# Ranking three quarters of the tokens early: seventeen expert tiles of layer 1 ahead of the last block's routing

## What is computed

```python
# attention half of layer 1: two-layer MLP behind the attention
h = relu(out @ W1 + b1); x = x + tanh(g_xattn[1]) * (h @ W2 + b2)
# expert half of layer 1, on xn = layernorm(x)
logits = xn @ Wg + bg
topk_vals, topk_idx = top_k(logits, 2)
topk_w = softmax(topk_vals)
h  = relu(xn @ W1[e] + b1[e])          # W1[e]: 256 x 512
eo = h @ W2[e] + b2[e]                 # W2[e]: 512 x 256
mixed = sum over the token's two experts of topk_w * eo
y = mixed + xn
x = x + tanh(g_ffn[1]) * (gamma * layernorm(y) + beta)
```

## Time and profile before

| | us |
|---|---|
| median of 3 runs | 1427.07 (1425.08 to 1428.34) |
| the profiled execution | 1421.31 |
| its span, first to last instruction | 1419.5 |
| TensorE busy | 1346.5 (95%) |
| ScalarE busy | 975.0 (69%) |
| VectorE busy | 597.7 (42%) |
| GpSimd busy | 175.8 (12%) |
| mean granted clock of TensorE | 0.986 |

### The profile page before, as it was taken

How to read it: one execution, slowest core, us unless ns; L and a number is a source line. 1 busy time by engine, 2 the same in 40 slices (tenths; PEclk the granted TensorE clock), 3 DMA queues, 4 the chain that set the end, 5 groups by cost and what they waited for, 6 DMA issues and landing times. The chain is left out here.

```text
span 1419.5 us, 33642 instructions
## 1 busy us (share of the span) xinstructions
PE 1346.5 (95%) x14020; PEld 741.4 (52%) x14020; DVE 597.7 (42%) x1257; ACT 975.0 (69%) x1190; POOL 175.8 (12%) x194
## 2 busy tenths in 40 slices
PE   7899999999999998999988999999999998899994
PEld 4433333333333555999953333334334338799973
DVE  7412143152333344334271222662662676544435
ACT  4699999999998233223268996996996980255532
POOL 2000000000000331233300000000000000276530
PEclk9999999999999999999999999999999999899997
DMA  7771010010100913311259110110111215022224
GB/s 212 176 124 29 21 28 21 25 25 17 32 24 21 312 66 96 123 49 50 74 123 197 39 28 17 35 29 17 35 29 50 68 35 175 27 72 72 72 69 162
DMA packets 66533, 101.96 MB, mean 72 GB/s; under 512 B 10476, under 2 KB 48626, under 8 KB 65484
## 3 DMA queue, kind: packets, MB, share of 16 engines
q1 hardware_dynamic: 60428, 83.53, 21.6%
q0 software_dynamic: 5952, 16.26, 3.6%
HBM read 69.04 MB, written 26.22 MB: 67 GB/s over the span
## 5 line engine op out<-in xcount | busy, mean ns | idle before, releaser
L1410 ACT ACTIVATE arena<-ps 128x1024 f32<-128x1024 f32 x536 | 535.3, 1195 | 37.1 <-PE ps L1123 36.5
L1123 PE MATMUL ps<-arena 99*32 99x512 bf16 x6528 | 450.0, 382 | 13.2 <-issue 6.4
L1123 PEld LDWEIGHTS ps<-arena 99*32 99x32 bf16 x6528 | 158.4, 95 | 384.6 <-issue 159.8
L1143 PE MATMUL ps<-arena 128*32 128x512 f32 x2240 | 355.8, 593 | 0.7 <-ACT xn L1403 0.4
L1410 ACT ACTIVATE wqkv<-ps 128x1024 f32<-128x1024 f32 x264 | 279.3, 1192 | 16.5 <-PE ps L1123 16.3
L1143 PE MATMUL ps<-wqkv,arena 128*32 128x512 f32 x1088 | 206.4, 593 | 0.1
L1508 DVE SCALAR_TENSOR_TENSOR work<-xn,last_v,ps 128x512 f32<-128x512 f32 x30 | 22.4, 748 | 307.3 <-PE ps L1143 307.2
L2005 PE MATMUL ps<-work,arena 128*128 128x128 f32 x1184 | 145.4, 279 | 3.0 <-DVE work L2097 1.6
L2005 PEld LDWEIGHTS ps<-work,arena 128*128 128x128 f32 x1184 | 144.3, 195 | 7.0 <-DVE work L2097 4.0
L1039 POOL DMA_INDIRECT work<-xn_img,fetch x62 | 60.4, 974 | 558.5 <-DVEq L1095 514.1
L2019 PE MATMUL ps<-arena,work 128*128 x496 | 117.2, 380 | 0.0
(11 more groups left out here) (228 smaller groups left out, 1289.3 us busy)
## 6 DMA issues: line engine op xcount, KB each, us to landing
arena<-in_ew SPq DMA_DIRECT2D x16, 512.0 KB, 5.8
arena<-q_img SPq DMA_DIRECT2D x32, 192.0 KB
arena<-y_tok SPq DMA_DIRECT2D x12, 512.0 KB, 6.5
arena<-k_img SPq DMA_DIRECT2D x8, 624.0 KB, 12.1
q_img<-work SPq DMA_DIRECT2D x18, 256.0 KB, 2.6
k_img<-work SPq DMA_DIRECT2D x21, 208.0 KB, 2.4
arena<-q_img SPq DMA_DIRECT2D x32, 128.0 KB
arena<-in_rg SPq DMA_DIRECT2D x8, 512.0 KB, 7.3
```

The lines of the kernel that those rows point to most:

```text
L1123: last = nc.tensor.matmul(ps[i * VW:(i + 1) * VW, buf + j, :], keys, q2[0:ROWS + SHIFT, h, :], start=True, stop=True, skip_group_check=True)
L1143: last = nc.tensor.matmul(ps[j * VW:(j + 1) * VW, 6 + g % 2, :], v_aug[:, c, HG * g + j, :], exps, start=(c == 0), stop=(c == NC - 1), ski ...
L1410: nc.scalar.activation(probs[n % RING], ps[:, buf:buf + 2, :], ACT.Exp, scale=SCALE).then_inc(s_exp, 1)
```

## The change

Layer 1 ranks the tokens of blocks 0 to 2 (24 of the 32 one-hot columns) by themselves. Of these 3072 pairs at least 24 - 7 = 17 tiles are full whatever the draw, and the first 17 full ones become tiles 0 to 16 of the loop. What is left over is ranked again, together with block 3, into 22 further tiles. The count of tiles stays 39.

- VectorE: in block 3 all eight experts' router products and `route` come before the third group; after it comes `rank_first`. `places` for the first lists follows the last group. `rank_rest` and its `places` follow the one-hots of block 3. Then the loop for tiles 17 to 38.
- TensorE: the first counts stand behind step 44 of block 3, the first lists behind attention, then 12 keep-warm products instead of 26, and after the projection the loop begins, in the same block. The last transpose, the last router product, the second counts and the second lists are put between tiles (after `down(0)`, `down(1)`, `down(3)` and `down(11)`). The other keep-warm products of layer 1 go.
- ScalarE: in tiles 0 to 16 it copies the rows, does bias and ReLU in four instructions per tile, and copies the result out (`first_scalar`), since VectorE is ranking. From tile 17 the loop is as before, but two diagonals follow each ReLU.
- GpSimd: in tiles 0 to 16 it adds the second bias. It fetches their rows from a second copy of the normalised rows, `xn_early`, of blocks 0 to 2.
- SP: writes that copy (three transfers of 512 KB), and loads `eb1` during the last block. The down weights are loaded where they were.

```diff
-FETCHED = [4, 1]
+FETCHED = [4, 0]
+COUNTS_AT = 44
...
+        self.early = self.top * (NB - 1) * TB if self.mlp else 0
+        self.first = self.early - E + 1 if self.mlp else 0
+        self.rest = self.tiles - self.first
...
-                    out=rows_in[i % ROWBUFS], out_offset=None, in_=xn_img[l],
+                    out=rows_in[i % ROWBUFS], out_offset=None, in_=xn_early if i < L.first else xn_img[l],
...
+            def first_scalar(act, between):
+                act.wait_ge(s_pl, 1)
+                act.wait_ge(s_eg, 16 * (E + 1))
+                copy_gate(act, 0)
+                copy_gate(act, 1)
...
+                def hidden(i):
+                    e = act.value_load(tile_e[0:1, i:i + 1], min_val=0, max_val=E - 1)
+                    act.wait_ge(s_gu, i + 1)
+                    if i >= 2:
+                        act.wait_ge(s_dn, i - 1)
+                    for f in range(4):
+                        last = nc.scalar.activation(hT[i % 2][:, f, :], ps[:, 2 + 2 * (i % 2), f * P:(f + 1) * P],
+                                                    ACT.Relu, bias=eb1[:, bass.ds(e, 1), f:f + 1]
+                                                    .rearrange("p a f -> p (a f)"))
+                    last.then_inc(s_h, 1)
...
+                copy_rows(0)
+                for i in range(L.first):
+                    if i + 1 < L.first:
+                        copy_rows(i + 1)
+                    hidden(i)
+                    if i:
+                        finish(i - 1)
+                    if i + 2 == L.first:
+                        act.wait_ge(s_pl, 2)
+                    copy_gate(act, i + 2)
+                    if i in between:
+                        between[i]()
+                finish(L.first - 1)
...
+                                elif b == NB - 1 and w == COUNTS_AT:
+                                    counts_first()
...
                     if l == 1:
-                        keep_warm(0, 26)
+                        lists_first()
+                        keep_warm(0, 12)
                         last_projection()
-                        keep_warm(0, 10)
-                        last_turn()
-                        last_logits()
-                        keep_warm(0, 11)
-                        counts()
-                        keep_warm(0, 55)
-                        lists()
-                        keep_warm(0, 12)
+                        for pair in range(2):
+                            pe.wait_ge(s_xup[pair], NB)
+                        loop_tensor(pe, {1: last_turn, 2: last_logits, 4: counts_rest, 12: lists_rest})
...
+                        last_block = l == 1 and b == NB - 1
...
+                        elif last_block:
+                            logits(b - 1, range(E))
+                            route(b - 1)
                         elif b:
                             logits(b - 1, range(E // 2))
                         group(b, 2)
-                        if b and l == 1:
+                        if b and l == 1 and not last_block:
...
                     if l == 1:
 
+                        rank_first()
```

More of the change, by code:

```diff
@@ L86, in __init__, with slot, pieces @@
         self.experts = E + (n == 0)
+        self.early = self.top * (NB - 1) * TB if self.mlp else 0
+        self.first = self.early - E + 1 if self.mlp else 0
+        self.rest = self.tiles - self.first
+    def slot(self, k, t):
+        early = (NB - 1) * TB
+        if not self.mlp:
+            return k * NT + t
+        return k * early + t if t < early else self.early + k * TB + t - early
+    def pieces(self):
+        early = (NB - 1) * TB
+        first = [(self.slot(k, 0), k, 0, early) for k in range(self.top)]
+        return first, first + [(self.slot(k, early), k, early, TB) for k in range(self.top)]
 def build(nc, a, out):
@@ L292, in build, with __init__ @@
         gamma, beta = wqkv[:, 3, 0:D], wqkv[:, 3, D:2 * D]
+        at = (E + TB) * D
+        rank_all = over_ctx[:, at:at + TS]
+        count_first, taken = over_ctx[:, at + TS:at + TS + E], over_ctx[:, at + TS + E:at + TS + 2 * E]
+        rest_turns = over_ctx[:, at + TS + 2 * E:at + TS + 2 * E + 32].bitcast(U32)
+        class Lists:
+            def __init__(self, region, at, scanned, slots, tiles):
+                self.slots, self.tiles, self.cols = slots, tiles, tiles + tiles % 2
+                self.scan = [None] * 2
+                for i in range(2):
+                    self.scan[i], at = view(region, at, [scanned, E])
+                self.val, at = view(region, at, [slots, E])
+                self.mask, at = view(region, at, [slots, E])
+                self.in_tile, at = view(region, at, [slots, self.cols], BF16)
+                self.token, at = view(region, at, [slots, 2 * self.cols], BF16)
+                self.in_row, at = view(region, at, [slots, P], BF16)
+                self.past, at = view(region, at, [tiles, E - 1])
+                self.end = at
+        L1 = layers[1]
+        first_lists = Lists(over_ctx, 0, L1.early, L1.early, L1.first)
+        rest_lists = Lists(arena, 14 * G, L1.top * TB, L1.slots, L1.rest)
         ps = ctx.enter_context(nc.psum_tensor("ps", [P, 8, 512], F32))
@@ L1220, in route, with counts_first @@
                                 last.then_inc(s_full7, 1)
+                    def counts_first():
+                        n = L.early
+                        pe.wait_ge(s_oh, NB - 1)
+                        pe.wait_ge(s_u, NB * NG - 1)
+                        nc.tensor.matmul(ps[:, 6, 0:n * E], below[:, :], oh[:, 0:n, :], start=True, stop=True,
+                                         skip_group_check=True)
+                        nc.tensor.matmul(ps[:, 6, n * E:2 * n * E], ones[:, :], oh[:, 0:n, :], start=True, stop=True,
+                                         skip_group_check=True).then_inc(s_cnt, 1)
                     max_tensor(pe)
@@ new lines, in places @@
+                    def places(of=None, bank=6, at=0):
+                        dve.wait_ge(s_list, 2 if at else 1)
+                        n, first, second = (NTL, 0, NTL + 1) if of is None else (of.tiles, LISTS_AT, LISTS_AT + of.cols)
+                        cols = slice(at, at + n)
+                        turn, row = ps[:, bank, first:first + n], ps[:, bank, second:second + n]
+                        chain(nc.vector.tensor_copy(pad[:, cols], turn))
+                        chain(nc.vector.scalar_tensor_tensor(out=code[:, cols], in0=row, scalar=float(NT),
+                                                             in1=pad[:, cols], op0=ALU.mult, op1=ALU.add))
+                        chain(nc.vector.tensor_scalar(pad[:, cols], code[:, cols], 0.0, pad_row[:, 0:1],
+                                                      ALU.is_equal, ALU.mult))
+                        chain(nc.vector.scalar_tensor_tensor(out=dest[:, cols], in0=code[:, cols], scalar=-1.0,
+                                                             in1=pad[:, cols], op0=ALU.add, op1=ALU.add))
+                        last = nc.vector.tensor_scalar(fetch[:, cols], dest[:, cols], S - 1, None, ALU.bitwise_and)
+                        if of is first_lists:
+                            chain(last)
+                            chain(nc.vector.tensor_scalar(rest_turns[:, 0:n], fetch[:, cols], 4, 2, ALU.logical_shift_right,
+                                                          ALU.logical_shift_left))
+                            last = nc.vector.tensor_tensor(fetch[:, cols], fetch[:, cols], rest_turns[:, 0:n],
+                                                           ALU.subtract)
+                        last.then_inc(s_pl, 1)
@@ L1749, in _ @@
-                    last.then_inc(s_tok, 1)
-                    past = view(work, 0, [NTL, E - 1])[0]
-                    chain(nc.vector.tensor_tensor(past, iota_tile[:, 0:NTL].unsqueeze(2).broadcast_to([P, NTL, E - 1]),
-                                                  end[:, 0:E - 1].unsqueeze(1).broadcast_to([P, NTL, E - 1]),
-                                                  ALU.is_ge))
-                    chain(nc.vector.tensor_reduce(tilef[:, 0:NTL], past, AX.X, ALU.add))
-                    nc.vector.tensor_copy(tile_e[:, 0:NTL], tilef[:, 0:NTL])
@@ L1779, in shared_hidden @@
+                    if l == 0:
+                        rank_all_tokens()
+                    else:
+                        rank_rest()
+                        places(rest_lists, 3, L.first)
                     def shared_hidden(b, f):
@@ new lines, in _ @@
+                    if l == 0:
+                        pool.wait_ge(s_img, 16 * NB)
+                        for i in range(FETCHED[l]):
+                            fetch_rows(pool, i)
+                    else:
+                        pool.wait_ge(s_ie, 16 * (NB - 1))
+                        loop_pool(pool)
+            if l == 0:
+                with nc.Block() as block:
+                    block.sync(loop_sync)
+                    block.tensor(loop_tensor)
```

(3 more changed lines are left out.)

796 lines of the change are left out of this document (478 added, 318 removed).

## The result

| | before | with the change |
|---|---|---|
| median, both on the same chip | 1427.7 (1425.08 to 1432.21, 4 runs) | 1407.54 (1405.02 to 1411.57, 4 runs) |
| the profiled execution | 1421.31 | 1407.0 |
| its span | 1419.5 | 1405.2 |
| mean granted clock of TensorE | 0.986 | 0.982 |

The change is faster, as forecast: ratio 0.9858 (1.4%), 95% interval 0.9835 to 0.988, 20 us by the medians. The forecast was 1407.3, range 1401 to 1417. But the number hides errors of about 5 us in each direction that cancel, and the rest of the document is mostly about those.

A forecast was written before the change was run, and what follows sets the result against it. Bound: the chain through VectorE's last group, MLP, normalisation and ranking before the loop, TensorE's 3.73 us per tile in it. 26.6 - 0.6 - 3.2 - 3.0 = 19.8 us gained, median 1407.3, range 1401 to 1417.

The forecast's parts named there:

- Work in front of the last group: VectorE, block 3: router products, routing and ranking of 24 columns before the last group make that path 6.7 us later.
- Clock in the projection: TensorE idles before the projection, which begins at 1.2 GHz and loses 2 us; bounds 0 and 4.
- Start of the loop: Update of x ends at 1199.6 and the loop starts there in place of 1226.24, 26.6 us earlier.
- Inside the first tiles: TensorE, loop start: block 3's transposing and logits come in, gate wait and low clock fall away; 0.6 us lost.
- Counts: TensorE, between loop tiles: the inserted second counts cost 0.4 us of its own time.
- Lists: TensorE, between loop tiles: the 32 inserted list matmuls cost 2.3 us of its own time.
- Change of hands at tile 17: TensorE, in the loop at tile 17: about 0.5 us lost.
- ScalarE's pace: First 17 tiles: ScalarE at 3.92 us per tile paces TensorE's 3.73; 3.0 lost over 15, bounds 0 and 10.6.
- rival 1: First 17 tiles: ScalarE pays every read and ReLU in full, 4.44 us per tile; 7.6 more, 1415; chance 0.20.
- rival 3: First tiles: each ScalarE ReLU waits for its register instruction, 5.7 us per tile; slower than before, 1434; chance 0.06.
- Rival 2: Neither ScalarE in the first tiles nor the projection's clock costs anything; 5.0 us less, 1402.3; chance 0.12.
- Rival 4: First down-projection waits for weights landing at 1204.3, wanted about 1204.9, no margin; with 10 us delay 1417; chance 0.05.

The follow-up runs named there:

- run 1: The changed kernel measured again with nothing edited: 1405.81 us, ratio to before 0.9846.
- Run 3: The change with 17 keep-warm products ahead of the first lists and 34 behind them in place of 12: 1403.27 us, ratio to before 0.9834.
- Run 4: run 2 with three more waited-for ScalarE copies of 256 columns in each of the first seventeen tiles: 1407.62 us, ratio 0.9858.
- run 2: The change with each of the second ranking's four in_row instructions waiting for one further up-projection (tiles 8 to 11): 1404.37 us, ratio to before 0.984.
- run 9: The change with its overlap alone undone, block 3's routing finished before the loop: 1434.15 us, ratio to before 1.002.
- run 5: The change with the edits of run 2 and Run 3 together: 1404.51 us, ratio 0.9835.
- run 7: run 2 with the last group right after attention, first list matmuls between the projection's halves, and 31 keep-warm products: 1397.95 us, ratio 0.9778.
- run 6: run 5 with SP issuing four experts' down weights and biases before the last gather: 1399.12 us, ratio 0.9794.

## Why the prediction was right

Taken in the order of its terms; times of the change less 5.53.

- **Work in front of the last group**: third group predicted 1152.6, measured 1152.6. Ranking predicted 15.2, measured 15.2. Last group predicted 1175.1, measured 1175.0: 6.6 later against 6.7 (the prediction's own terms add up to 1175.0, 6.5 later, where it writes 1175.1 and 6.7). Each piece had a near row.
- **Clock in the projection**: 2.0 predicted, 0 to 4 the bounds, 2.9 measured in the change (10.03 for 7.14) and 1.7 in run 1. Run 3 shows that it is the clock: with TensorE busy it is 0. The row at full clock after 1.66 us of idle did not carry over to 4.33 and 3.80 us. The Trainium skill (TensorE: Matmul & The Clock Gate, Part 1) says that the throttled rate is the default and that an idle stretch returns the engine to it. The trace agrees: the windows above show 0.69, 0.72 and 0.60 before it is 1.00 again.
- **Start of the loop**: 1199.6 predicted, 1205.97 less 5.53 is 1200.4; 25.8 earlier, not 26.6. The difference is the clock's.
- **Inside the first tiles**: 0.6 predicted, 1.0 measured (14.5 from the first transposes to the up-projection of tile 3). Counts 0.4 predicted, 0.4 measured. Lists 2.3 predicted, 0.8 measured: the 0.72 for eight stands in a stretch at a granted clock of 0.84 to 0.50 and has 80 columns, where these 44 columns run at full clock. Change of hands at tile 17: 0.5 predicted, 0 measured (from the up-projection of tile 13, at 1263.04, to that of tile 38, at 1356.41, 25 tiles take 93.4, 3.73 each).
- **ScalarE's pace**: the one step whose mechanism failed. "Sum 3.92 against TensorE's 3.73: ScalarE paces these tiles, and over 15 of them 3.0 is lost." Nothing is lost. Run 4 measured its work at 2.97 a tile at most. Piece by piece, start to start in that run: copy and read of the number 0.72 where 0.82 was put, ReLUs 1.01 for 1.45, result copy and next read 0.26 for 0.7, gate copy 0.95 as predicted. A single ReLU does last 0.36, as predicted, but the next one starts 0.25 after it, and the read before the gate copy runs beside the instruction in front of it when the engine is behind. The row that said so was at hand (no idle before ScalarE's gate copy) and was used only against rival 1.
- **Not foreseen**: the 3.9 us of the held fetch. The prediction checked that GpSimd "stays under 3.7" by its own instructions, and did not ask what VectorE's four wide writes at the same time would do to them. Runs 1, 2 and 3 show it; it costs 2.2 where the clock stays up (run 1) and 3.9 where it falls.

The sum in measured terms is 25.8 - 1.0 - 0.4 - 0.8 - 0 - 3.9 = 19.7, and from the second group to the last down-projection's end the two traces give 250.7 and 231.3, 19.5 gained against 19.8 forecast. The lists (1.5 too much), the handover (0.5) and ScalarE (3.0) add up to 5.0, and the late start (0.8, the clock's), the first tiles (0.4) and the held fetch (3.9) took 5.1. The mechanism of the gain was right, and run 9 confirms its size; the closeness of the number was luck.

Of the rivals, 1 and 3 (ScalarE's upper bounds) are refuted by the ScalarE rows and by run 4. Rival 2 was right for ScalarE and wrong for the clock. Rival 4, the weights, is no 10 us, but it is real: the change waits 0.48 in one profile and 1.86 in the other, and in runs 3, 4, 5 and 7 it waits 2.0 to 2.5 us. "No margin" was right, but its working was off twice: the last bias of before landed 6.7 after the start of its issue, at 1196.4, while the prediction counted from the end of the issue; and in the change it landed 9.0 after the start of its issue, at 1206.0 shifted, 9.7 later than before and not 6.7. What slowed the loads was not tested.

## What to carry to other kernels

When work is moved so that two engines run side by side for the first time, check each pair for interference, not only each engine's sum of busy time: here VectorE's long writes stretched GpSimd's short instructions five- to sevenfold, and one instruction per tile instead of four in a row made that harmless. When a start is moved forward, list what it will find not ready next (the clock, then the weights, then the fetched rows), since each mend alone, as in runs 3 and 5, is handed on to that wait. A read of the expert number that shows as idle time on an engine that isn't behind can be latency that vanishes when it is: make the engine the slowest, as run 4 did, before adding such idle to its pace.

## What the runs showed of the hardware

- GpSimd is held while VectorE runs `in_row` (a comparison of two fp32 operands from SBUF, 1024 columns, bf16 out). A GpSimd DMA issue that met four of them in a row took 5.04 and 4.88 us in place of 0.96, an addition 4.97 in place of 0.73; an instruction that met a single piece took 1.4 to 2.1 (runs 2, 5 and 6). GpSimd did not get in between the four pieces. In all three profiles the held instruction ended 0.6 to 0.85 us after the small two-operand instruction behind the pieces (in the change 1247.71 and 1248.55), which is about its own length. VectorE is held in turn: beside the addition at 1240.46 one of its instructions on 128x264 took 0.85 us where the next of the same shape took 0.42. The Trainium skill (SBUF — State Buffer, Who interferes with whom) says that a VectorE instruction with two SBUF inputs contends with a GpSimd instruction that reads SBUF, because its second input comes through a read interface that the two share. The additions agree. The same section infers that making DMA descriptors needs the write interface, so that such a VectorE instruction would not stall it. The indirect DMA issues here were held as long as the addition. They also take their row numbers from SBUF, and no run here tells whether it was that reading or the making of descriptors that was held.
- ReLUs on ScalarE of 128 columns out of PSUM, with the bias addressed by a register, last 0.36 us each and start 0.25 us apart, and the register instructions between them cost nothing visible.
- Reading an expert number into a register of ScalarE shows as 0.26 to 0.33 us of idle behind a short instruction. Before the gate copy it disappears when the engine is behind (0.67 against 0.26 from the start of one copy to the start of the next); before the ReLUs it stayed 0.33 in the one run that put ScalarE behind (run 4).
